# The first layer's kept operands read back in four transfers per half step instead of seven

## The chip, the cores and the metric

The kernel runs on one core of one Trainium2 chip. The metric is the device time of one execution in microseconds (us), lower being better.

## The reference, cut to what matters

Two batch rows of 2048 tokens with 512 features go through three small two-layer networks (two shared ones, one chosen by an id per batch row). A softmax gate weighs the three, the result is added to the tokens, and a second block adds one 512x512 product chosen by a category id.

```
x = hidden_states                                  # [2, 2048, 512]
s0 = relu(x @ swi[0]) @ swo[0]                     # 512 -> 2048 -> 512
s1 = relu(x @ swi[1]) @ swo[1]
eo = relu(x @ wi[type_label]) @ wo[type_label]     # per batch row
w = softmax(relu(concat(eo[:,0], s0[:,0], s1[:,0]) @ g1) @ g2)
x = x + eo * w[:,0] + s0 * w[:,1] + s1 * w[:,2]
x = x + (x @ W[cat_ids] + b[cat_ids])
```

The change touches only how the operands of the first layer (`swi`, `wi`), once prepared, reach TensorE. What is computed stays the same.

## The kernel before, in words

**Tiling.** The 4096 tokens are taken in four supers of 1024 (two blocks of 512). In a super, each of the three networks is worked in four steps of 512 hidden features, so there are 4 x 12 = 48 steps `N`, and each step has two half steps `n = 2N, 2N+1` of 256 hidden features, 96 in all. A half step multiplies 2x2 blocks by a scheme of seven block products in place of eight. Its seven "up" products (`up(n, i)`, i = 0 to 6, L1769) read the operand tile `WU[:, i]`, a high and a low part of 256 columns each, and the token operands `XH`, `XL`. Each product is two groups of three 512-column matmuls (high x high, high x low, low x high), six in all. A step's second layer has seven "down" products of twelve matmuls each, which read `WD`, a ring of four slots, and the hidden operands `HH`, `HL`.

**Operands made once, kept in DRAM.** The seven operands of a half step are sums of weight blocks, split in high and low parts on ScalarE and VectorE. This is done for the steps that `prepared(N)` names: all twelve of super 0, and the four steps of the third network in super 2 (steps 32 to 35), whose weights belong to the other batch row. They are then stored: `keep_up` (L446) writes a half step's operands 0 to 2 and then 3 to 6 from `WU` to `wu_kept`, `keep_down` (L473) writes one `WD` slot to `wd_kept`. The other 32 steps, 64 half steps, read them back: `load_up(n, i)` (L479) brings one operand of 256 KB, `load_down` (L488) one `WD` slot of 512 KB. `WU` has one buffer: operand i of half step n may be overwritten once product i of half step n-1 has ended (`s_up`).

**The order of the work.** Every engine walks the same hand-written loop: for each step `m` seven iterations i. In one iteration TensorE does two up products, j = 2i and 2i+1 (products 0 to 6 of half step `a = 2(m+1)`, then 0 to 6 of `b = a+1`), and one down product (the sum of it is added into `ACC` by VectorE). SyncE issues nearly all transfers, from one queue of instructions and in this order within an iteration: the keeps of up operands if steps are being prepared, the loads that follow up products 2i and 2i+1 (L652 to L655), in the last two steps of a super also a token operand (`load_operand`, L544, and `load_tokens`), then a `load_down`, spills of sums, `keep_down` of slots just made, and the rest. Each issue may be preceded by waits, and while SyncE waits, all that is behind it waits too.

VectorE makes the low parts (`down_low`, L1294, which a `keep_down` waits for through `s_wld`), the low parts of tokens (`token_low`, L1278), sums of hidden blocks and the additions of down products. TensorE waits in `up` for the operand's own semaphore, `s_wu[i]`, one for each of the seven (L1790).

**Where the two regimes meet.** After step 11 and after step 35 prepared steps end and steps with loads begin. During m = 11 and m = 35 SyncE's queue holds the last `keep_down`s of the prepared step between the first `load_up`s. These are the loads for half steps 25, 26 and for 73, 74.

Of the kernel before, what the change touches and what calls it, by code (L numbers as in the profile page):

```python
# [5 lines left out]
F32 = mybir.dt.float32  # L6
# [18 lines left out]
HALVES = 2 * STEPS  # L25
# [11 lines left out]
PRODUCTS = 7  # L37
# [2 lines left out]
UP_BANK = [0, 2, 1, 0, 1, 2, 1]  # L40
UP_ANEW = [True, True, False, False, False, False, False]
EARLY = 3

DN_PAIR = [0, 0, 1, 0, 1, 0, 1]
DN_ANEW = [True, False, False, True, False, False, False]
# [22 lines left out]
def super_of(N):  # L68
    return N // STEPS_SUPER


def net_of(N):
    return N % STEPS_SUPER // STEPS_NET


def slice_of(N):
    return N % STEPS_NET


def prepared(N):  # L80

    return 0 <= N < STEPS and (super_of(N) == 0 or (super_of(N) == 2 and net_of(N) == 2))


def prepared_half(n):
    return prepared(n // 2)


def weight_set(N):
    return net_of(N) * STEPS_NET + slice_of(N) + (STEPS_NET if net_of(N) == 2 and super_of(N) >= 2 else 0)  # L90
# [5 lines left out]
PREP_HALF = [sum(prepared_half(i) for i in range(n)) for n in range(HALVES + 1)]  # L96
# [88 lines left out]
def x_index(s, i):  # L185
    return (X_ORDER if s > 0 else X_ORDER_FIRST).index(i)
# [34 lines left out]
def build(nc, xT, expert_id, category_id, wi, wo, swi, swo, g1, g2, W, bias, out):  # L221
# [6 lines left out]
    wu_kept = nc.dram_tensor("wu_kept", [2 * SETS, P, PRODUCTS, 2, HB], F32, kind="Internal").ap()  # L228
# [6 lines left out]
    with ctx:  # L235
        def sem(name):
            return ctx.enter_context(nc.semaphore(name))
# [3 lines left out]
        def sb(name, shape, dt=F32, at=None):  # L241
            size = 4
            for n in shape[1:]:
                size *= n
            offset = place[0] if at is None else at
            t = nc.alloc_sbuf_tensor_at(name, shape, dt, offset=offset)
            if at is None:
                place[0] += (size + 63) // 64 * 64
            return t
# [14 lines left out]
        WU = sb("WU", [P, PRODUCTS, 2, HB], F32R)  # L264
# [85 lines left out]
        s_wld = sem("down_low_parts")  # L350
        s_wuk = [sem("up_kept_early"), sem("up_kept_late")]
        s_wdk = [sem(f"down_kept_{r}") for r in range(WD_SLOTS)]
        s_wu = [sem(f"up_operand_loaded_{i}") for i in range(PRODUCTS)]
        s_wd = [sem(f"down_operand_loaded_{r}") for r in range(WD_SLOTS)]
        s_up = sem("up_product")
        s_dn = sem("down_product")
# [62 lines left out]
        def _(sp):  # L419
# [26 lines left out]
            def keep_up(n, late):  # L446
                part = slice(EARLY, PRODUCTS) if late else slice(0, EARLY)
                sp.wait_ge(s_wlu, 4 * PREP_HALF[n] + 2 + 2 * late)
                sp.dma_start(wu_kept[2 * weight_set(n // 2) + n % 2, :, part, :, :],
                             WU[:, part, :, :].bitcast(F32)).then_inc(s_wuk[late], 16)  # L450
# [26 lines left out]
                             WD[:, r, :, :, :].bitcast(F32)).then_inc(s_wdk[r], 16)  # L477

            def load_up(n, i):  # L479
                late = int(i >= EARLY)  # L480
                sp.wait_ge(s_up, PRODUCTS * (n - 1) + i + 1)
                sp.wait_ge(s_wuk[late], 16 * PREP_HALF[n])
                if weight_set(n // 2) == 0:
                    sp.wait_ge(s_wsk, 64)
                sp.dma_start(WU[:, i, :, :].bitcast(F32),
                             wu_kept[2 * weight_set(n // 2) + n % 2, :, i, :, :]).then_inc(s_wu[i], 16)

            def load_down(N, i):  # L488
                e = down_of(N, i)
# [14 lines left out]
            def load_tokens(s, j):  # L504

                k, h = ((0, 0), (1, 0), (1, 1), (0, 1))[j]
                if j < 3:
                    if s > 0:
                        sp.wait_ge(s_xlo, PRODUCTS * s)
                        sp.wait_ge(s_gpart, KD * (3 * (s // 2) + (2 if s % 2 else 0)))  # L510
                        for q in range(4):
                            sp.wait_ge(s_ak[q], 16 * (1 if s == 1 else SUPERS - 1))
                        if s > 1:
                            sp.wait_ge(s_out, 16 * SLICES * (s - 1))
                    dst = XS[:, j, :]
                elif s > 0:
                    sp.wait_ge(s_up, PRODUCTS * (2 * STEPS_SUPER * s - 1) + 4)
                    dst = XT[:, 3, :]
                else:
                    dst = first_B21  # L520
                sp.dma_start(dst, xT[s, :, k, h, :]).then_inc(s_xs[j], 16)
# [24 lines left out]
            def load_operand(s, i):  # L546

                q = {1: 0, 4: 1, 2: 2, 5: 3}[i]
                sp.wait_ge(s_up, PRODUCTS * (2 * STEPS_SUPER * s - 1) + i + 1)
                sp.wait_ge(s_ak[q], 16 * s)  # L550
                sp.dma_start(XT[:, i, :], xT_kept[s - 1, q, :, :]).then_inc(s_xt[i], 16)
# [77 lines left out]
            for m in range(STEPS):  # L629
# [4 lines left out]
                for i in range(PRODUCTS):  # L634
# [16 lines left out]
                        keep_up(b + 1, 0)  # L651
                    for j in (2 * i, 2 * i + 1):  # L652
                        n = a + j // PRODUCTS
                        if n + 1 < HALVES and not prepared_half(n + 1):
                            load_up(n + 1, j % PRODUCTS)  # L655
                        if end and j == PRODUCTS + 3:
                            load_tokens(s + 1, 3)
                        elif end and PRODUCTS < j < 2 * PRODUCTS - 1:
                            load_operand(s + 1, j - PRODUCTS)
# [222 lines left out]
        def _(act):  # L882
            def token_high(s, i):
                if s > 0:
                    act.wait_ge(s_up, PRODUCTS * (2 * STEPS_SUPER * s - 1) + i + 1)
                _, _, (sums, fourth), _ = x_from[i]
                if s > 0 and i in s_xt:
                    act.wait_ge(s_xt[i], 16 * s)
                elif sums:
                    act.wait_ge(s_xT, sums)  # L890
                elif fourth:
                    act.wait_ge(s_x4, 1)
                else:
                    act.wait_ge(s_xs[x_loaded[i]], 16 * (s + 1))
                act.activation(XH[:, i, :], x_source(s, i), ACT.Copy).then_inc(s_xhi, 1)  # L895

            def up_high(n, late):
                if n > 2:
                    act.wait_ge(s_up, PRODUCTS * (n - 1) + (PRODUCTS if late else EARLY))
                    act.wait_ge(s_wuk[late], 16 * PREP_HALF[n])  # L900
# [860 lines left out]
        def _(pe):  # L1761
            def product(dst, stationary, moving, start, stop):
                pairs = ((0, 0), (0, 1), (1, 0))
                for j, (a, c) in enumerate(pairs):
                    ins = pe.matmul(dst, stationary[a], moving[c], start=start and j == 0, stop=stop and j == 2,  # L1765
                                    skip_group_check=True)
                return ins

            def up(n, i):  # L1769
                N = n // 2  # L1770
                if i == 0:
                    pe.wait_ge(s_relu, 4 * (n - 1) + 1)
                if i == 1 and n == 2:
                    pe.wait_ge(s_relu, 4 * (n - 1) + 2)
                elif i == 1:
                    pe.wait_ge(s_ev, 2 * (n - 2))
                if i == 2:
                    pe.wait_ge(s_p1, n - 1)
                if i == 4:
                    pe.wait_ge(s_u, n - 1)  # L1780
                if i == 5:
                    pe.wait_ge(s_w, n - 1)
                if i == 6:
                    pe.wait_ge(s_ev, 2 * (n - 2) + 1)
                if n == 2 or n % (2 * STEPS_SUPER) == 0:
                    pe.wait_ge(s_xlo, PRODUCTS * super_of(N) + x_index(super_of(N), i) + 1)
                if prepared_half(n):
                    pe.wait_ge(s_wlu, 4 * PREP_HALF[n] + (1, 2, 2, 3, 4, 4, 4)[i])
                else:
                    pe.wait_ge(s_wu[i], 16 * (n - PREP_HALF[n] + 1))  # L1790
                for q in range(2):
                    cols = slice(q * P, (q + 1) * P)
                    toks = slice(q * TB, (q + 1) * TB)
                    ins = product(ups[UP_BANK[i]][:, :], (WU[:, i, 0, cols], WU[:, i, 1, cols]),
                                  (XH[:, i, toks], XL[:, i, toks]), q == 0 and UP_ANEW[i], q == 1)
                ins.then_inc(s_up, 1)
# [171 lines left out]
```

## Time and profile before

| what | value |
|---|---|
| median of 3 runs | 1934.02 us (1933.66 to 1934.57) |
| the profiled execution, device time | 1933.93 us |
| its span in the profile | 1931.9 us |
| TensorE matmuls busy | 1927.0 us (100%), 8494 of them |
| VectorE busy | 1356.0 us (70%) |
| ScalarE busy | 980.0 us (51%) |
| GpSimd busy | 344.8 us (18%) |
| DMA, all queues | 470.91 MB, mean 244 GB/s |
| DMA queue of SyncE, share of 16 engines | 71.1% |

How to read it: the span runs from the first to the last instruction of the program in the profiled execution; the device time of that same execution is 2.0 us longer. Busy shares are shares of the span. The matmuls are pipelined, and each record lasts longer (389 ns) than the distance from one start to the next, so that "busy" merges them: the idle time of TensorE is what is left between merged stretches.

### The profile page before, as it was taken

To read this page: it belongs to the slowest core of one execution; us is meant where nothing else is said; L and a number is where in the kernel's file an instruction comes from. 1 tells how busy PE (TensorE), PEld (TensorE's weight loads), DVE (VectorE), ACT (ScalarE), POOL (GpSimd) and SP (SyncE) were. 2 spreads that over 40 slices of the span, in tenths; PEclk is the share of its full clock that TensorE was granted. 3 is DMA by queue.
4 is the path that set the end of the run, shared out by engine and by line. 5 is a ranking of instruction groups with operands and counts; after the bars stand their busy time and mean duration, and the time that the engine had idled before them with its cause. 6 is when DMAs were issued, how large, how long until landed. Compare 5 with 4: busy or idle time off the path is not lost. (4 is left out here: it accounts for less than half of the span.)

```text
span 1931.9 us, 25225 instructions
## 1 busy us (share of the span) xinstructions
PE 1927.0 (100%) x8494; PEld 1593.8 (82%) x8494; DVE 1356.0 (70%) x1523; ACT 980.0 (51%) x1441; POOL 344.8 (18%) x245
## 2 busy tenths in 40 slices
PE   9999999999999999999999999999999999999999
PEld 8888888888888888888888888888888888888887
DVE  8999999998666556665655545589976666555566
ACT  7666756766553334444554344456566434344342
POOL 0221132123111111331111111111321112111120
PEclk9999999999999999999999999999999999999999
DMA  6868777867877666886776676587788677656652
GB/s 234 326 251 325 288 293 269 310 242 306 295 250 232 205 217 186 279 290 228 243 253 212 202 225 197 194 287 290 268 304 282 221 234 226 213 183 213 223 158 99
DMA packets 193314, 470.91 MB, mean 244 GB/s; under 512 B 17060, under 2 KB 58020, under 8 KB 187044
## 3 DMA queue, kind: packets, MB, share of 16 engines
q1 hardware_dynamic: 192900, 468.52, 71.1%
q8 instruction: 70, 1.15, 0.2%
q10 hardware_dynamic: 288, 0.79, 0.1%
q14 instruction: 56, 0.46, 0.1%
HBM read 322.44 MB, written 146.80 MB: 243 GB/s over the span
## 5 line engine op out<-in xcount | busy, mean ns | idle before, releaser
L1765 PE MATMUL rps<-HH,WD 128*128 128x512 f32 x2672 | 876.8, 389 | 0.0
L1765 PE MATMUL ups<-XH,WU 128*128 128x512 f32 x2632 | 864.7, 389 | 0.3 <-DMA WU<-wu_kept 0.3
L1765 PEld LDWEIGHTS rps<-HH,WD 128*128 128x128 f32 x2672 | 501.6, 188 | 104.7 <-issue 0.5
L1765 PEld LDWEIGHTS ups<-XH,WU 128*128 128x128 f32 x2632 | 493.9, 188 | 104.5 <-issue 0.9
L1765 PE MATMUL rps<-HL,WD 128*128 128x512 f32 x1336 | 519.9, 389 | 0.0
L1765 PE MATMUL ups<-XL,WU 128*128 128x512 f32 x1316 | 512.2, 389 | 0.0
L802 POOL TENSOR_TENSOR HT<-hid 128x512 f32<-128x512 f32 x81 | 111.2, 1373 | 1349.2 <-PE rps L1765 1349.2
L1311 DVE TENSOR_TENSOR HL<-HT,HH 128x1024 fp32r<-128x1024 f32 x240 | 290.0, 1217 | 11.4 <-ACT HH L988 6.3
L1333 DVE SCALAR_TENSOR_TENSOR ACC<-rps,gw,ACC 128x1024 f32<-128x1024 f32 x126 | 161.5, 1282 | 192.7 <-PE rps L1765 192.5
L1765 PEld LDWEIGHTS rps<-HL,WD 128*128 128x128 f32 x1336 | 250.7, 188 | 52.1
L1765 PEld LDWEIGHTS ups<-XL,WU 128*128 128x128 f32 x1316 | 247.1, 188 | 51.2
L988 ACT ACTIVATE HH<-HT 128x1024 fp32r<-128x1024 f32 x240 | 252.6, 1054 | 24.7 <-DVE HT L802 23.5
L1330 DVE TENSOR_TENSOR ACC<-rps,ACC 128x1024 f32<-128x1024 f32 x124 | 151.1, 1219 | 89.2 <-PE rps L1765 89.0
L964 ACT ACTIVATE HT<-HT 128x512 f32<-128x512 f32 x94 | 59.4, 632 | 269.7 <-DVE HT L1361 269.7
L1311 DVE TENSOR_TENSOR HL<-hid,HH 128x1024 fp32r<-128x1024 f32 x96 | 131.8, 1373 | 20.7 <-ACT HH L988 20.7
L1352 DVE TENSOR_TENSOR hid<-ups,w 128x512 f32<-128x512 f32 x94 | 64.6, 687 | 110.0 <-PE ups L1765 109.8
L956 ACT ACTIVATE hid<-ups 128x512 f32<-128x512 f32 x94 | 55.9, 595 | 109.8 <-PE ups L1765 109.8
L948 ACT ACTIVATE u<-ups 128x512 f32<-128x512 f32 x94 | 56.2, 598 | 102.9 <-PE ups L1765 102.9
L942 ACT ACTIVATE w<-ups 128x512 f32<-128x512 f32 x94 | 55.2, 588 | 97.0 <-PE ups L1765 97.0
L988 ACT ACTIVATE HH<-hid 128x1024 fp32r<-128x1024 f32 x96 | 101.7, 1059 | 3.5 <-PE rps L1765 2.0
L1003 ACT ACTIVATE rps<-rps 128x512 f32<-128x512 f32 x96 | 55.5, 582 | 83.9 <-PE rps L1765 68.6
L936 ACT ACTIVATE ups<-ups 128x512 f32<-128x512 f32 x94 | 54.8, 583 | 76.2 <-PE ups L1765 73.0
(155 smaller groups left out, 1530.9 us busy)
## 6 DMA issues: line engine op xcount, KB each, us to landing
WU<-wu_kept SPq DMA_DIRECT2D x448, 256.0 KB, 3.6
WD<-wd_kept SPq DMA_DIRECT2D x224, 512.0 KB, 3.5
wd_kept<-WD SPq DMA_DIRECT2D x112, 512.0 KB, 4.0
wu_kept<-WU SPq DMA_DIRECT2D x30, 1024.0 KB, 4.9
wu_kept<-WU SPq DMA_DIRECT2D x30, 768.0 KB, 4.1
sums_kept<-ACC SPq DMA_DIRECT2D x28, 512.0 KB, 6.0
MB<-sums_kept SPq DMA_DIRECT2D x28, 512.0 KB, 5.6
XS<-in_x_dram SPq DMA_DIRECT2D x20, 512.0 KB, 6.2
```

What stands on the lines that cost most here:

```text
L802: eng.tensor_tensor(dst, p, q, op).then_inc(s_T[half], 1)
L942: act.activation(w[:, :], ups[2][:, :], ACT.Copy).then_inc(s_w, 1)
L948: act.activation(u[:, :], ups[1][:, :], ACT.Copy).then_inc(s_u, 1)
L956: act.activation(hid[:, 0, half, :], ups[0][:, :], ACT.Relu).then_inc(s_relu, 1)
L964: act.activation(HT[:, 1, n % 2, :], HT[:, 1, n % 2, :], ACT.Relu).then_inc(s_relu, 1)
L988: act.activation(HH[:, i, :, :], src, ACT.Copy).then_inc(s_hhi, 1)
L1003: act.activation(rps[1][:, j, :], rps[0][:, j, :], ACT.Copy).then_inc(s_pc, 1)
L1311: dve.tensor_tensor(HL[:, i, :, :], src, HH[:, i, :, :].bitcast(F32), ALU.subtract).then_inc(s_hlo, 1)
L1330: dve.tensor_tensor(ACC[:, j, :, :], src[:, :, :], ACC[:, j, :, :], ALU.add).then_inc(s_acc, 1)
L1333: dve.scalar_tensor_tensor(out=ACC[:, j, :, :], in0=src[:, :, :], scalar=gw[:, g:g + 1], in1=ACC[:, j, :, :], op0=ALU.mult, op1=ALU.add).t ...
L1352: dve.tensor_tensor(hid[:, 2, half, :], ups[1][:, :], w[:, :], ALU.add).then_inc(s_ev, 1)
L1765: ins = pe.matmul(dst, stationary[a], moving[c], start=start and j == 0, stop=stop and j == 2, skip_group_check=True)
```

## The change

Four semaphores take the place of seven. A transfer now brings operand 0 alone, or operands 1 and 2, 3 and 4, or 5 and 6 together. It is issued where the later operand's load stood, after the later product of the previous half step has ended; the calls for products 1, 3 and 5 are gone. TensorE's wait before product i is for the semaphore of the transfer that brings it.

```diff
+PAIRS = 4
...
-        s_wu = [sem(f"up_operand_loaded_{i}") for i in range(PRODUCTS)]
+        s_wu = [sem(f"up_operands_loaded_{i}") for i in range(PAIRS)]
...
             def load_up(n, i):
                 late = int(i >= EARLY)
+                part = slice(max(i - 1, 0), i + 1)
                 sp.wait_ge(s_up, PRODUCTS * (n - 1) + i + 1)
                 sp.wait_ge(s_wuk[late], 16 * PREP_HALF[n])
                 if weight_set(n // 2) == 0:
                     sp.wait_ge(s_wsk, 64)
-                sp.dma_start(WU[:, i, :, :].bitcast(F32),
-                             wu_kept[2 * weight_set(n // 2) + n % 2, :, i, :, :]).then_inc(s_wu[i], 16)
+                sp.dma_start(WU[:, part, :, :].bitcast(F32),
+                             wu_kept[2 * weight_set(n // 2) + n % 2, :, part, :, :]).then_inc(s_wu[i // 2], 16)
...
                     for j in (2 * i, 2 * i + 1):
                         n = a + j // PRODUCTS
-                        if n + 1 < HALVES and not prepared_half(n + 1):
+                        if n + 1 < HALVES and not prepared_half(n + 1) and j % PRODUCTS % 2 == 0:
                             load_up(n + 1, j % PRODUCTS)
...
                 else:
-                    pe.wait_ge(s_wu[i], 16 * (n - PREP_HALF[n] + 1))
+                    pe.wait_ge(s_wu[(i + 1) // 2], 16 * (n - PREP_HALF[n] + 1))
```

## Rows read from the trace of the kernel before

**Rows 1.** The profile page, part 1, busy time of each engine.
```profile
PE 1927.0 (100%) x8494; PEld 1593.8 (82%) x8494; DVE 1356.0 (70%) x1523; ACT 980.0 (51%) x1441; POOL 344.8 (18%) x245
```

**Rows 2.** Who waited for whom, TensorE (total us, times, longest).
```profile
PE ups L1894 <- POOL ones L854: 1.0, 1, 1.0
PE ups L1765 <- DMA WU<-wu_kept: 0.3, 1, 0.3
PE aps L1765 <- DVE XL L1730: 0.2, 1, 0.2
```

**Rows 3.** Chain of waits: start, us, what; then stretches (PE, PEld, DVE, ACT, POOL; clock, DMA, GB/s).
```profile
1541.67 2.72 PE ups L1765 x12
1544.39 2.72 PE rps L1765 x12
...
1917.80 10.89 PE rps L1765 x48
...
600.00:700.00 100.00, 100.00 (x443) 82.82 (x442) 63.88 (x63) 41.67 (x59) 14.18 (x10) 1.00 0.70 221
1900.00:1932.00 32.00, 28.51 (x125) 22.86 (x123) 16.96 (x20) 3.39 (x4) 0.00 (x0) 0.99 0.18 66
```

**Rows 4.** DMA issues (count, KB, median to landing), then tile WU's landing times.
```profile
WU<-wu_kept SPq DMA_DIRECT2D x448, 256.0 KB, 3.6
WD<-wd_kept SPq DMA_DIRECT2D x224, 512.0 KB, 3.5
...
DMA to landing us min/median/max: 2.6/3.9/11.2
```

**Rows 5.** Who waited for whom, SyncE's queue.
```profile
SPq L496 <- PE rps L1765: 500.4, 217, 5.0
SPq L485 <- PE ups L1765: 390.4, 368, 3.7
SPq L476 <- DVE WD L1298: 277.3, 100, 13.7
```

**Rows 6.** SyncE's issues in order of time, end of step m = 34 and step m = 35.
```profile
1391.33 0.37 SPq L485 DMA_DIRECT2D WU<-wu_kept  x1
1391.79 0.39 SPq L551 DMA_DIRECT2D XT<-xT_kept  x1
1392.29 0.43 SPq L485 DMA_DIRECT2D WU<-wu_kept  x1
...
1407.44 1.28 SPq L485 DMA_DIRECT2D WU<-wu_kept  x2
1422.35 0.32 SPq L476 DMA_DIRECT2D wd_kept<-WD  x1
1422.77 1.21 SPq L485 DMA_DIRECT2D WU<-wu_kept  x2
1424.03 0.47 SPq L476 DMA_DIRECT2D wd_kept<-WD  x1
1424.60 1.58 SPq L485 DMA_DIRECT2D WU<-wu_kept  x2
```

**Rows 7.** TensorE in order of time, half step 73's products 1 and 2.
```profile
1426.15 0.39 PE L1765 MATMUL ups<-XH,WU 128*128 128x512 f32 x1
...
1427.28 0.39 PE L1765 MATMUL ups<-XH,WU 128*128 128x512 f32 x1
...
1427.94 0.47 PE L1765 MATMUL ups<-XH,WU 128*128 128x512 f32 x1 [0.27 <-DMA WU<-wu_kept]
...
1428.25 0.40 PE L1765 MATMUL ups<-XL,WU 128*128 128x512 f32 x1
```

**Rows 8.** Chain of waits at 1422.77; tile WU, the loads issued at 1423.24 and 1424.60.
```profile
1422.77 5.04 DMA WU<-wu_kept
...
L485 SPq DMA_DIRECT2D WU<-wu_kept x1: 732/732/732, 1423.2 to 1423.2; - x1
...
DMA to landing us min/median/max: 5.2/5.2/5.2
...
L485 SPq DMA_DIRECT2D WU<-wu_kept x1: 371/371/371, 1424.6 to 1424.6; - x1
...
DMA to landing us min/median/max: 5.7/5.7/5.7
```

**Rows 9.** Step m = 11: SyncE 464.59 (landing beside it), TensorE from 467.96.
```profile
464.59 1.21 SPq L485 DMA_DIRECT2D WU<-wu_kept  x2
...
DMA to landing us min/median/max: 4.6/4.6/4.6
...
467.96 0.39 PE L1765 MATMUL ups<-XH,WU 128*128 128x512 f32 x1
```

**Rows 10.** VectorE from 1401.86 (21 records up to 1422.84, idle only before the first); TensorE at 1409.60.
```profile
1401.86 1.71 DVE L1282 TENSOR_TENSOR XL<-XT,XH 128x1024 fp32r<-128x1024 f32 x1 [1.49 <-ACT XH L895]
...
1410.31 1.21 DVE L1330 TENSOR_TENSOR ACC<-rps,ACC 128x1024 f32<-128x1024 f32 x1
...
1421.64 0.68 DVE L1298 TENSOR_TENSOR WD<-PDS,WD 128x512 fp32r<-128x512 f32 x1
...
1409.60 0.39 PE L1765 MATMUL rps<-HH,WD 128*128 128x512 f32 x1
```

## The prediction

> **What bounds the kernel now.** The page comes first: matmuls cover 1927.0 of the 1931.9 us, and VectorE follows at 70% [rows 1]. Next, what TensorE waited for: 1.5 us over three waits, one of them for an operand of the change, 0.3 us [rows 2]. Then its pace. Twelve matmuls take 2.72 us in mid-kernel, and 48 take 10.89 us in the last stretch: 227 ns each both times, although the DMA engines are busy 0.70 of the time in the one and 0.18 in the other [rows 3]. So the pace does not hang on the load on the DMA engines, and 8494 x 0.227 = 1928 us is practically the span. The granted clock is 1.00 at mid-kernel and 0.99 at the end. Nothing is to be won but those waits; what the change can do is make an operand late.
>
> **Count.** The 448 loads of 256 KB [rows 4] become 64 of 256 KB and 192 of 512 KB, the bytes unchanged. SyncE saves 192 issues of 0.3 to 0.4 us, which is worth nothing: outside the places below it spends its time waiting for products [rows 5]. Waits of TensorE stay one per product.
>
> **The ordinary half step.** The operands with odd numbers are now fetched one product later, and the even one of a pair is no earlier. Of a pair, the first operand counts, since it is needed first. An iteration is two up products and a down product, 2 x 2.72 = 5.44 us [rows 3]. Operand 1 of half step b is used at the start of iteration 4, and its old contents are free after half step a's product 1, in iteration 0. That leaves one down product and three iterations, 2.7 + 16.3 = 19.0 us. The pair waits for product 2, a down and an up product later: 19.0 - 2.7 - 1.4 = 14.9 us. In the other parity the window is 15.0 us. The median landing is 3.6 us for 256 KB and 3.5 us for 512 KB [rows 4]; the longest of all transfers of `WU`, keeps included, took 11.2 us [rows 4]. So the pair is hidden wherever SyncE issues on time. Cost 0; the cover is these 15 us, and with the cover gone each late us costs TensorE a us.
>
> **Where SyncE does not issue on time.** SyncE waited for VectorE's low parts at `keep_down` for 277.3 us in 100 waits, the longest 13.7 us [rows 5]. Most of it lies in prepared steps, where no load is behind. The exceptions are steps m = 11 and m = 35. At m = 35 (half step 73) loads 0 and 1 are issued in iteration 0, at 1407.44. Then `keep_down` blocks the queue for some 14 us, and goes at 1422.35. Loads 2 and 3 follow at 1422.77 and 1423.24 [rows 6, 8]. Operand 2 lands 5.04 us after its issue, 1427.81, and that is the wait of 0.3 us: product 2's first matmul starts at 1427.94 instead of 1427.28 + 0.23 = 1427.51, so 0.43 us is lost [rows 7, 8]. The change moves load 1 across this `keep_down`, from 1407.44 to 1422.77, joined to load 2. But product 1 starts at 1426.15 [rows 7], 1.36 us ahead of product 2.
>
> **When the pair lands.** No row shows this transfer. Load 3, issued 0.47 us behind load 2, lands 5.2 us after its issue, at 1428.45, 0.64 us behind load 2 [rows 8]. The pair has exactly the bytes of loads 2 and 3 and the same `keep_down` in front, so I take load 3's landing, 1428.4. From below the bound is load 2's own landing, 1427.8 (as if the doubled size cost nothing). From above, the load at 1424.60, with more in front, took 5.7 us [rows 8]; with 0.6 for the doubled size that is 6.3 us, landing 1429.1.
>
> **What comes earlier.** At the end of m = 34 the token operand at 1391.79 stands behind load 1 of half step 72 [rows 6]. The pair now comes behind it, so it has 256 KB less in front, which is up to 0.64 us. VectorE idles 1.49 us for that operand at 1401.86 and then works without a pause to the low part at 1421.64 that frees the `keep_down` [rows 10]. Such a lead passes through all of this but one: the addition at 1410.31 needs a down product whose last matmul runs 1409.60 to 1409.99 [rows 10], so 0.3 us is left. I take 0.3; the bounds are 0 and 0.6.
>
> **The sum.** At m = 35: landing 1428.4 - 0.3 = 1428.1, 0.13 us to the matmul as now (1427.81 to 1427.94), start 1428.2. Stall 1428.2 - 1426.15 = 2.1 us, less the 0.43 already lost: +1.7 us. At m = 11 the same queue: load 2 issued at 464.59 landed 4.6 us later, 469.2, just in time; the pair lands 0.6 later and 0.3 earlier, 469.5, start 469.6; product 1 starts at 467.96 [rows 9]. Stall 1.7 us, less about 0.1 for the slower matmul there now: +1.6 us. Sum +3.3 us. The pairs 3-4 and 5-6 behind them are not late: pair 3-4 goes at 1424.60 and lands, by the load of that moment, 5.7 us later at 1430.3, while product 3, an up product and a down product behind 1427.94, starts near 1432.0, and later still by the stall. Nothing gives a stall back: VectorE gets time that it does not need, and all later loads shift with TensorE. For the clock I allow nothing, since no stretch read shows less than 0.99 [rows 3]; the stall of now slows only the next matmul, by 0.08 us (1427.94 to 1428.25) [rows 7]. The profiled execution took 1933.93 us, 0.1 below the median of the runs: 1933.93 + 3.3 = 1937.2 us. With the low ends (landing as load 2, 0.3 earlier) the stalls are about 0.6 shorter each: +2.0, 1936.0. With the high ends (6.3 us, no lead) it is 2.6 + 3.0 = +5.6, 1939.5.
>
> A page speaks for the change: the Trainium skill, DMA: Bandwidth & Descriptors, under Bandwidth (Measured), advises batching transfers to 1 MiB or more, and under Anatomy of one DMA gives each a fixed cost of about 2 us. By that rule three fixed costs per half step go, so the pair would come sooner than two loads. No row agrees: two loads 0.47 us apart land 0.64 us apart [rows 8], so fixed parts overlap in the queue.
>
> **Rivals.** A measurement of this kernel can tell 0.2%, 3.9 us, from no change.
>
> (a) Slower by more: the lead of 0.3 us does not arrive, or the queue in front of the pair is longer, so that it lands at load 3's time or after it. Price: 1428.45 + 0.13 - 1426.15 - 0.43 = 2.0 and 469.8 + 0.13 - 467.96 - 0.1 = 1.9, so +3.9 at least and +5.6 at most: 1937.9 to 1939.5. It decides once the pair lands 0.3 us later than I take it at both places. For it: all transfers at these moments stand in a full queue. Against it: VectorE's idle 1.49 us is plainly that token transfer's. Chance 0.33.
>
> (b) Hidden: the pair lands before product 1, or VectorE's lead is much larger, since the order in front of it changes. It needs a landing 2 us sooner than taken, under 3.4 us from issue, where the rows show 4.6 and 5.04. Time 1934.0, down to 1933.4 if the 0.5 us of now goes too. Chance 0.09.
>
> (c) Faster: TensorE's pace is held back by the transfers of small rows after all, and a share of it returns. By [rows 3] the pace at a DMA share of 0.18 is that at 0.70, so I give it 0.04; one per cent of the pace would give 1915. By the page's rule, too, no more than the 0.5 us of waits could return, since TensorE has no other idle time for a load; its time would be 1933.4.
>
> (d) That the change does not do what it says can hardly be: call, slice and semaphore index agree.
>
> **How the numbers follow.** Forecast (two stalls, +2.0 to +3.8) 0.54, (a) 0.33, (b) 0.09, (c) 0.04. Both the forecast and (b) lie within 0.2%: same 0.63. Slower 0.33, faster 0.04. The likeliest time is 1937.2 us. The range takes the forecast and (a) nearly whole and leaves out (c), most of (b) and the end of (a): 1934.6 to 1939.3.
>
> **What would show it.** TensorE's waits for `WU` rise from 0.3 to some 4 us, in two waits near 468 and 1426, each before the first matmul of a product 1 and none before product 2. In SyncE's queue one load of 256 KB stands at 1407.4, and the pair behind the `keep_down` at about 1422.5 (1422.8 would be (a)), landing about 5.6 us later. The addition at 1410.31 starts at 1410.0, with a short idle time in front. Between these places the matmuls keep 2.72 us per twelve. The prediction is wrong if there is no wait at those places, if waits appear in ordinary half steps, or if the pace changes.

## The result and the profile after

Twelve executions of the changed kernel took 1939.89 us in the median (1937.86 to 1941.31), twelve of the kernel before 1934.23 us (1933.66 to 1935.08). The ratio is 1.0026 with a 95% interval of 1.0018 to 1.0033, so slower, by about 5 us (5.7 us between the two medians). The profiled execution took 1938.38 us (span 1936.3 us), 1.5 us under the median, and that difference turned out to be part of the answer: the times of the changed kernel lie in two groups. The four executions with a mean granted TensorE clock of 1.000 took 1937.86 to 1938.60 us, the eight with 0.999 took 1939.63 to 1941.31 us.

The profile page of the changed kernel, parts 1 and 5 (busy, mean ns of one, then idle before and its releaser):

```profile
PE 1927.6 (100%) x8494; PEld 1593.4 (82%) x8494; DVE 1359.5 (70%) x1523; ACT 980.2 (51%) x1441; POOL 344.7 (18%) x245
...
L1770 PE MATMUL ups<-XH,WU 128*128 128x512 f32 x2632 | 864.7, 389 | 4.0 <-DMA WU<-wu_kept 3.9
```

Who waited for whom, TensorE, changed kernel:

```profile
PE ups L1770 <- DMA WU<-wu_kept: 3.9, 2, 2.2
...
PE rps L1815 <- ACT WD L1053: 0.4, 1, 0.4
```

The busy time is that of before [rows 1] to within a microsecond, and so is the matmul (389 ns). What is new is idle time in one group, two waits for `WU` with 3.9 us in place of one with 0.3 [rows 2]. Here are the two places, TensorE in order of time in the changed kernel, last matmul of a down product and then product 1:

```profile
467.86 0.39 PE L1770 MATMUL rps<-HH,WD 128*128 128x512 f32 x1
469.92 0.47 PE L1770 MATMUL ups<-XH,WU 128*128 128x512 f32 x1 [1.67 <-DMA WU<-wu_kept]
...
1428.07 0.39 PE L1770 MATMUL rps<-HH,WD 128*128 128x512 f32 x1
1430.69 0.47 PE L1770 MATMUL ups<-XH,WU 128*128 128x512 f32 x1 [2.23 <-DMA WU<-wu_kept]
```

A matmul normally starts 0.23 us after its forerunner, so product 1 was due at 468.09 and at 1428.30: stalls of 1.83 and 2.39 us. The bracket shows less, since it counts only idle time behind the modelled end of the last matmul. Less what stood there before (0.43 and 0.08), that is 3.7 of the 4.45 us between the two profiled executions. Another 0.3 us is the wait at L1815 near the start, which lasts anything from nothing (the kernel before, `own_25`) to 1.8 us (`own_73`) in the profiles of this document, and 0.4 us is a short wait for VectorE near 1520.

SyncE's queue around the two places, changed kernel:

```profile
464.26 0.32 SPq L479 DMA_DIRECT2D wd_kept<-WD  x1
464.69 0.37 SPq L490 DMA_DIRECT2D WU<-wu_kept  x1
...
1409.74 0.39 SPq L490 DMA_DIRECT2D WU<-wu_kept  x1
...
1424.64 0.32 SPq L479 DMA_DIRECT2D wd_kept<-WD  x1
1425.07 0.37 SPq L490 DMA_DIRECT2D WU<-wu_kept  x1
```

One load at 1409.74 where there were two [rows 6], and operand 1 now comes after the blocking `keep_down`, fifteen us later. Elsewhere nothing is late. DMA issues and a mid-kernel stretch of the changed kernel (columns as in [rows 4] and [rows 3]):

```profile
WD<-wd_kept SPq DMA_DIRECT2D x224, 512.0 KB, 3.4
WU<-wu_kept SPq DMA_DIRECT2D x192, 512.0 KB, 4.3
...
600.00:700.00 100.00, 100.00 (x443) 82.81 (x442) 65.21 (x65) 41.41 (x58) 15.05 (x10) 1.00 0.69 221
```

A pair takes 4.3 us to land in the median where a single one took 3.6, and 443 matmuls in 100 us is what it was.

### The profile page after: what moved, and what is told of

It is laid out like the page before. It is cut to its first block and busy times, and to the rows that moved or that the text cites. A ratio compares the mean times of both kernels' runs of the same rounds, so it can differ in the third digit from the quotient of the medians.

```text
span 1936.3 us, 24841 instructions
## 1 busy us (share of the span) xinstructions
PE 1927.6 (100%) x8494; PEld 1593.4 (82%) x8494; DVE 1359.5 (70%) x1523; ACT 980.2 (51%) x1441; POOL 344.7 (18%) x245
```

## The experiments

Every kernel ran with the kernel before on the same chip. Ratios are to it, with 95% intervals.

**The changed kernel again**, for its profile and its spread.

> The changed kernel, once more, for its profile and the spread of its times. First theory (two stalls, and after them in some executions a fall of TensorE's clock): executions fall in two groups, near 1938.3 us with a granted clock of 1.000 and near 1940 us with 0.999; the two waits for WU are 1.7 and 2.2 us in both. Rival (something spread over the kernel, at 64 half steps): the times are one group, and the twelve matmuls of an ordinary product pair take more than 2.72 us.

Median 1938.15 us against 1933.77, ratio 1.0023 (1.0014 to 1.0033). Six executions with clock 1.000 took 1936.85 to 1938.47 us, four with 0.999 took 1939.48 to 1940.76: two groups again, as expected. The profiled one is of the second kind, 1940.46 us. Its stretches, then TensorE in order of time behind its second stall:

```profile
1426.00:1430.00 4.00, 3.72 (x17) 2.75 (x15) 4.00 (x6) 3.49 (x5) 0.00 (x0) 1.00 0.82 219
1430.00:1432.00 2.00, 0.34 (x2) 0.33 (x3) 2.00 (x3) 1.15 (x3) 0.00 (x0) 1.00 0.98 389
1432.00:1435.00 3.00, 3.00 (x9) 2.35 (x8) 2.41 (x3) 0.60 (x1) 0.00 (x0) 0.50 1.02 419
1435.00:1440.00 5.00, 5.00 (x23) 4.07 (x22) 0.96 (x1) 0.60 (x1) 0.91 (x1) 0.96 1.02 399
```

```profile
1429.33 0.39 PE L1770 MATMUL rps<-HH,WD 128*128 128x512 f32 x1
1431.66 0.47 PE L1770 MATMUL ups<-XH,WU 128*128 128x512 f32 x1 [1.94 <-DMA WU<-wu_kept]
1431.97 0.58 PE L1770 MATMUL ups<-XL,WU 128*128 128x512 f32 x1
1432.35 1.06 PE L1770 MATMUL ups<-XH,WU 128*128 128x512 f32 x2
1433.20 0.63 PE L1770 MATMUL ups<-XL,WU 128*128 128x512 f32 x1
...
1435.62 0.40 PE L1770 MATMUL ups<-XL,WU 128*128 128x512 f32 x1
```

After the wait the granted clock is 0.50, the lower of the two levels (1.2 GHz), and matmuls follow each other at 0.43 us (0.85 for two, 1432.35 to 1433.20) in place of 0.23. Nine matmuls take 1435.62 - 1431.97 = 3.65 us where 2.04 would do, so this costs 1.6 us more. The first stall of the same execution (469.00 to 471.35 less one step of 0.23, 2.12 us) left the clock alone. The Trainium skill, TensorE: Matmul & The Clock Gate, Part 1, says that a TensorE that was idle is throttled to 1.2 GHz until it has been active again. The trace agrees at the second stall (2.10 us, 0.50 after it) and not at the first (2.12 us, 1.00 after it), so the length of the stall alone does not decide it here.

**Operand 1 alone in its old place, at the two half steps only** (`own_both`). All other half steps keep their pairs. `load_alone` is the old load of operand 1, with a semaphore of its own, on which product 1 waits.

```diff
+SPLIT = (25, 73)
...
-                part = slice(max(i - 1, 0), i + 1)
+                part = slice(2, 3) if i == 2 and n in SPLIT else slice(max(i - 1, 0), i + 1)
...
+                        if n + 1 in SPLIT and j % PRODUCTS == 1:
+                            load_alone(n + 1)
```

> The changed kernel, but for half steps 25 and 73 operand 1 comes alone, in its old place ahead of the keep_down, and operand 2 alone in its old place; the 62 other half steps keep their pairs. Two stalls: the time is that of the kernel before, 1934.2 us within 0.4, with the wait of 0.3 us before product 2 of half step 73 back, and no execution has a clock under 1.000. Rival (pairs cost at every half step, by their later fetch or their size): 1937 us or more stays, of the 5.7 us at most 4.2 go.

Median 1934.06 us against 1933.77, ratio 1.0001 (0.9992 to 1.0010), no execution under 1.000. TensorE's only wait for `WU` is that of before:

```profile
...
PE ups L1782 <- DMA WU<-wu_kept: 0.2, 1, 0.2
```

The 62 half steps with pairs cost 0.3 us by the medians, which cannot be told from nothing (the interval is 1.5 us below to 1.9 us above); the 4.4 us of the changed kernel on this chip come from the two.

**One place each.** `SPLIT = (25,)` leaves the stall at half step 73, `SPLIT = (73,)` that at 25.

> The changed kernel, but at half step 25 operands 1 and 2 come apart, operand 1 ahead of the keep_down; half step 73 keeps its pair, so one stall is left, of 2.0 to 2.4 us, less the 0.4 us that stands there anyway. Two stalls that add: 1934.0 + 1.8 = 1935.8 us where the clock stays at 1.000, and 1.7 us more, 1937.5 us, in the executions with 0.999, a third to a half of them. Rival (the fall of the clock needs both stalls, or is no work of them): no execution with 0.999, or as many as with both.

> The mirror of it: half step 25 keeps its pair and stalls 1.8 to 2.1 us, half step 73 has its operands apart. Two stalls that add: 1935.9 us with the clock at 1.000, 1937.6 us with 0.999. The gains of this and of the other, taken together, make the whole of what the change lost. Rival (one place starts what the other pays for): one of the two kernels is at 1934 us and the other at 1938 us.

Against 1933.79 us: the first 1936.35 us, ratio 1.0013 (1.0004 to 1.0022), the second 1936.14 us, 1.0012 (1.0003 to 1.0021). Each loses 2.4 to 2.6 us, together 4.9, between the 4.4 us of the changed kernel in its second set of runs and the 5.7 of the first. So the places add, and one stall alone can bring the clock down (against the rival that both are needed): four of eleven executions of the first have 0.999 (1937.42 to 1937.88 us), two of the second, where two more at 1937.42 and 1937.81 us show 1.000 in three digits. Six of 22 with one stall against 12 of 22 with both fits falls that come from each stall by itself, but the numbers are too small to show it. The profiled execution of the second is one with a fall, behind a stall of 2.00 us at half step 25 that ended at 470.39. There the clock stayed up for about a microsecond after TensorE had resumed, 0.88 being the mean of the first stretch:

```profile
470.00:472.00 2.00, 1.61 (x6) 1.38 (x7) 2.00 (x3) 0.00 (x0) 0.00 (x0) 0.88 1.03 412
472.00:474.00 2.00, 2.00 (x6) 1.53 (x5) 1.26 (x2) 0.60 (x1) 0.00 (x0) 0.50 1.03 422
474.00:480.00 6.00, 6.00 (x25) 4.92 (x25) 1.22 (x1) 1.50 (x3) 2.10 (x2) 0.92 1.02 363
```

**The pair asked for ahead of the keep_down** (`early`).

```diff
+                        if m in (11, 35) and j == 2:
+                            continue
                         if n + 1 < HALVES and not prepared_half(n + 1) and j % PRODUCTS % 2 == 0:
                             load_up(n + 1, j % PRODUCTS)
+                        if m in (11, 35) and j == 0:
+                            load_up(n + 1, 2)
```

> The changed kernel with its pairs, but in steps 11 and 35 the pair 1-2 is issued in iteration 0, ahead of the keep_down that blocks the queue, once product 2 has ended. Two stalls by queue position: the pair is asked for some 10 us sooner, both waits go, and so does the 0.3 us wait of the kernel before: 1933.6 us, 0.3 to 0.7 below before. Rival (the size of a transfer or its wait for the later product is what costs): a stall of a us or more stays, 1936 us or more.

Median 1933.62 us against 1933.77, ratio 0.9997 (0.9988 to 1.0006), so equal; the 0.3 to 0.7 us below before that I expected are too small to be seen. SyncE's queue in step 35 and TensorE's waits:

```profile
1408.14 3.91 SPq L490 DMA_DIRECT2D WU<-wu_kept  x2
1423.04 1.52 SPq L479 DMA_DIRECT2D wd_kept<-WD  x2
1424.68 1.56 SPq L490 DMA_DIRECT2D WU<-wu_kept  x1
```

```profile
PE rps L1819 <- ACT WD L1057: 1.2, 1, 1.2
PE ups L1903 <- POOL ones L863: 1.0, 1, 1.0
PE aps L1774 <- DVE XL L1739: 0.2, 1, 0.2
```

Same sizes, same wait for product 2, and no wait for `WU` at all: it is the place in the queue that cost.

**Place without size** (`late1`): the kernel before, with operand 1 of the two half steps moved behind the `keep_down`, 256 KB as ever.

```diff
+                        if n + 1 in (25, 73) and j % PRODUCTS == 1:
+                            continue
+                        if n + 1 in (25, 73) and j % PRODUCTS == 2:
+                            load_up(n + 1, 1)
```

> The kernel before with its seven transfers; only operand 1 of half steps 25 and 73 is issued after the keep_down, directly ahead of operand 2, each still 256 KB. By place alone: operand 1 lands where operand 2 did (4.6 and 5.0 us after the issue), stalls of 1.4 and 1.8 us before product 1, operand 2 then in time: 1934.2 + 1.4 + 1.4 = 1937.0 us, plus up to 1.8 us in executions in which the clock falls. By size (the rival: only joining them stalls): 1934.5 us at most.

Median 1936.44 us, ratio 1.0013 (1.0004 to 1.0022), no execution under 1.000 (1935.35 to 1937.39). TensorE at both places:

```profile
468.01 0.39 PE L1769 MATMUL rps<-HH,WD 128*128 128x512 f32 x1
469.51 0.47 PE L1769 MATMUL ups<-XH,WU 128*128 128x512 f32 x1 [1.11 <-DMA WU<-wu_kept]
...
1427.49 0.39 PE L1769 MATMUL rps<-HH,WD 128*128 128x512 f32 x1
1428.44 0.47 PE L1769 MATMUL ups<-XH,WU 128*128 128x512 f32 x1 [0.56 <-DMA WU<-wu_kept]
```

Stalls of 1.27 and 0.72 us before product 1, the second shorter than the 1.8 I expected, since operand 1 landed 4.0 us after its issue there and not 5.0. Less the 0.51 us that stood there before, they make 1.5 us, while the profiled execution (1935.81 us) lies 2.0 us above the median of before, and the median 2.7 us above it. That this is near the 2.8 of the expectation is luck: the stalls that were seen do not add up to it, and what the slower executions add was not profiled. The move costs a stall without any joining; joining adds to it (1.83 and 2.39). No execution here shows a mean clock under 1.000.

**Another grouping** (`group01`): 0-1, 2-3, 4-5, 6.

```diff
-                part = slice(max(i - 1, 0), i + 1)
+                part = slice(i - 1 if i % 2 else i, i + 1)
...
-                        if n + 1 < HALVES and not prepared_half(n + 1) and j % PRODUCTS % 2 == 0:
+                        if n + 1 < HALVES and not prepared_half(n + 1) and j % PRODUCTS in (1, 3, 5, 6):
...
-                    pe.wait_ge(s_wu[(i + 1) // 2], 16 * (n - PREP_HALF[n] + 1))
+                    pe.wait_ge(s_wu[i // 2], 16 * (n - PREP_HALF[n] + 1))
```

> The changed kernel with another grouping, still four transfers: 0-1, 2-3, 4-5 and 6 alone, each after its later product. Now operand 1 stands ahead of the keep_down, and the pair 2-3 behind it lands 0.6 us after operand 2 alone would, while product 2 is due 1.36 us later than product 1. By the place of a pair's first operand: stalls of 0.6 us (half step 25) and 1.0 us (73) before product 2, none before product 1, 1933.8 + 0.6 + 0.6 = 1935.0 us, and no fall of the clock. Rival (any pair behind the keep_down costs what 1-2 did): 1937 us or more.

Median 1935.10 us against 1933.78, ratio 1.0006 (0.9997 to 1.0015), all eleven at 1.000. TensorE, last matmul of product 1 and first of product 2:

```profile
469.22 0.39 PE L1770 MATMUL ups<-XH,WU 128*128 128x512 f32 x1
470.14 0.47 PE L1770 MATMUL ups<-XH,WU 128*128 128x512 f32 x1 [0.53 <-DMA WU<-wu_kept]
...
1428.13 0.39 PE L1770 MATMUL ups<-XH,WU 128*128 128x512 f32 x1
1429.54 0.47 PE L1770 MATMUL ups<-XH,WU 128*128 128x512 f32 x1 [1.03 <-DMA WU<-wu_kept]
```

Stalls of 0.7 and 1.2 us, before product 2 this time. As many transfers as in the change, of the same sizes, for 1.3 us in place of 4.4 to 5.7: what matters is when the first operand of the pair behind the `keep_down` is due.

**A longer stall** (`longer`): the pair one `keep_down` further back.

```diff
+                        if m in (11, 35) and j == 2:
+                            continue
...
                     for k in made_after(past, which):
                         keep_down(k // PRODUCTS, k % PRODUCTS)
+                    if m in (11, 35) and i == 1:
+                        load_up(a + 1, 2)
```

> The changed kernel with the pair 1-2 of half steps 25 and 73 one keep_down further back in the queue: issued some 1.2 us later with 512 KB more in front, so that each stall grows from about 2.1 to about 3.5 us. If a longer stall makes the fall of the clock surer: every execution has 0.999 or less, and the time is 1934.0 + 3.5 + 3.1 + one or two times 1.7 = 1942.3 to 1944.0 us. Rival (the fall comes or not whatever the length of the stall): the executions stay split as before, with a median of 1941 us or less.

Median 1943.95 us, five executions from 1941.56 to 1945.69, ratio 1.0050 (1.0036 to 1.0064), all with 0.997 to 0.999. In the profiled one the first stall is 3.3 us, near the 3.5 that I had worked out, and the second 4.6 us, a microsecond more. The second:

```profile
1430.00:1434.00 4.00, 1.66 (x8) 1.04 (x6) 4.00 (x6) 3.19 (x6) 0.00 (x0) 1.00 0.99 277
1434.00:1440.00 6.00, 3.88 (x9) 3.13 (x10) 2.53 (x3) 0.60 (x1) 0.00 (x0) 0.51 1.01 391
```

Here the clock was at its lower level before TensorE resumed (1436.12). So falls go with the length of the stalls: a mean clock of 0.999 is absent from the 33 executions of `own_both`, `early` and `late1` (stalls up to 1.3 us), is there in part of those with stalls near 2 us, and in all five of this kernel. It does not take such a stall, though: one of the 92 executions of the kernel before shows 0.999 too, at 1936.41 us, the slowest of them. It was not profiled, so what lowered the clock there is open.

**The lead that did not come** (`xt_after`): at the end of steps 10 and 34 the pair goes ahead of the first token operand (and no more at j = 9).

```diff
...
+                        if m in (10, 34) and j == 8:
+                            load_up(n + 1, 2)
```

> The changed kernel, but at the end of steps 10 and 34 the pair 1-2 of half steps 24 and 72 is issued ahead of the first token operand, not behind it, so that this operand lands 1.3 us later. The forecast's term (VectorE passes a lead or a delay of that operand on, up to 0.3 us of lead): VectorE reaches the addition after its third token operand later, the keep_down that frees the queue goes 0.6 us or more later, both stalls grow by that. Rival (a collision of VectorE with GpSimd takes the lead away whatever the operand's landing): the keep_down goes within 0.2 us of where it does in the changed kernel, measured from the same product of TensorE, and the stalls stay at 1.7 to 2.4 us.

One execution, 1937.91 us, clock 1.000. SyncE's queue:

```profile
464.42 0.32 SPq L479 DMA_DIRECT2D wd_kept<-WD  x1
```

Product 1 was due at 468.06 here, so the `keep_down` goes 3.64 us ahead of it; in the changed kernel 468.09 - 464.26 = 3.83, in the kernel before 467.96 - 464.16 = 3.80. At half step 73 the figures are 3.68 us here and 3.66 in the changed kernel. VectorE's start on the token operand moved by 1.5 us between the two paired kernels and the queue by 0.2 and 0.0, so the rival has it. The stalls were 2.30 and 2.00 us; the first grew by 0.5 although the queue moved by only 0.2, as the pair landed 5.4 us after its issue and not 5.1. VectorE's rows show why the queue hardly moved. The kernel before, then the changed kernel, then `xt_after`:

```profile
443.67 1.72 DVE L1282 TENSOR_TENSOR XL<-XT,XH 128x1024 fp32r<-128x1024 f32 x1 [1.48 <-ACT XH L895]
...
448.73 1.22 DVE L1282 TENSOR_TENSOR XL<-XT,XH 128x1024 fp32r<-128x1024 f32 x1
449.86 1.21 DVE L1330 TENSOR_TENSOR ACC<-rps,ACC 128x1024 f32<-128x1024 f32 x1
```

```profile
442.98 1.28 DVE L1287 TENSOR_TENSOR XL<-XT,XH 128x1024 fp32r<-128x1024 f32 x1 [0.67 <-ACT XH L900]
...
447.61 2.32 DVE L1287 TENSOR_TENSOR XL<-XT,XH 128x1024 fp32r<-128x1024 f32 x1
449.85 1.21 DVE L1335 TENSOR_TENSOR ACC<-rps,ACC 128x1024 f32<-128x1024 f32 x1
```

```profile
444.45 2.30 DVE L1291 TENSOR_TENSOR XL<-XT,XH 128x1024 fp32r<-128x1024 f32 x1 [2.19 <-ACT XH L904]
...
448.99 1.21 DVE L1291 TENSOR_TENSOR XL<-XT,XH 128x1024 fp32r<-128x1024 f32 x1
450.12 1.21 DVE L1339 TENSOR_TENSOR ACC<-rps,ACC 128x1024 f32<-128x1024 f32 x1
```

With the change VectorE starts 0.7 us earlier and is still ahead at 447.61. Then the next token operand takes 2.32 us instead of 1.22, and the addition starts at 449.85 as before. GpSimd runs 512-column operations beside it that stretch too, first the kernel before, then the changed one:

```profile
443.02 1.29 POOL L810 TENSOR_TENSOR PDS<-PDR 128x512 f32<-128x512 f32 x1
```

```profile
443.14 2.28 POOL L815 TENSOR_TENSOR PDS<-PDR 128x512 f32<-128x512 f32 x1
```

In these rows the engine that starts first takes its short time and the other is stretched: VectorE at 442.98 (1.28 us) ahead of GpSimd at 443.14 (2.28), GpSimd at 443.02 (1.29) ahead of VectorE at 443.67 (1.72), and in `xt_after` GpSimd at 444.38 (1.28) ahead of VectorE at 444.45 (2.30). At half step 73 the lead goes at once. The token operand of 1401.86 before [rows 10] reads in the changed kernel:

```profile
1403.59 2.27 DVE L1287 TENSOR_TENSOR XL<-XT,XH 128x1024 fp32r<-128x1024 f32 x1 [1.27 <-ACT XH L900]
```

Product 1 is due 2.15 us later there (1428.30 against 1426.15), so VectorE starts 0.42 us early by that measure; the operation then takes 2.27 us in place of 1.71 and ends 0.14 us late, which is what the `keep_down` shows. That the collision is the cause of the lost lead fits all three traces; it was not tried without GpSimd.

**A version better than both?** The kernel before with its operands 2 and 3 asked for early (`before_early`), and the paired one again.

> The kernel before with its seven transfers; in steps 11 and 35 operands 2 and 3 are issued in iteration 0, ahead of the keep_down. The only wait of TensorE for WU goes: 0.3 to 0.5 us below the kernel before, 1933.4 us, the same as with pairs asked for early. Rival (pairs themselves give or take something): it differs from the paired kernel by 0.5 us or more.

> The paired kernel whose pair 1-2 is issued ahead of the keep_down, once more on the same chip as the two others: 1933.4 us, within 0.3 us of the seven transfers with the same early issue; lower than the kernel before by 0.2 to 0.5 us if the waits it lacks are all that differs. Rival: at or above the kernel before.

1933.82 us and 1933.73 us against 1933.78, ratios 1.0000 (0.9991 to 1.0009) and 0.9999 (0.9990 to 1.0008). Neither profile has a wait for `WU` left. All three are equal within what can be measured: both expected gains of 0.2 us or more are not seen, and the scatter of the start (0 to 1.8 us at the wait for ACT `WD` alone, from profile to profile) is larger than the 0.5 us at stake.

## Why the prediction was right or wrong

- **TensorE is the bound and its pace does not hang on transfers**: right. 443 matmuls in 100 us before and after, at a DMA share of 0.70 and 0.69, and `own_both` with 62 of 64 half steps paired is within 0.3 us of before.
- **Ordinary half steps cost nothing**: right as far as the times can tell, by the same run and by `early`, which has all its pairs.
- **Two stalls, at half steps 73 and 25, before product 1, none before product 2**: right, in place and kind; `own_25` and `own_73` show that they add.
- **When the pair lands**: right. 464.69 to 469.78 is 5.1 us (taken 5.2), 1425.07 to 1430.55 is 5.5 us (taken 5.6).
- **The lead of 0.3 us**: wrong. It was 0.03 us at half step 25, and at 73 the `keep_down` went 3.66 us ahead of product 1's due time where it had gone 3.80 us ahead, so 0.14 us later. The step that failed was "Such a lead passes through all of this but one": VectorE's operations were taken at fixed durations, and one of them was stretched, 2.32 us in place of 1.22 at half step 25 and 2.27 in place of 1.71 at 73. With that the stalls were 1.83 and 2.39 us against 1.7 and 2.1, and the sum +3.7 against +3.3. This is the upper edge of the forecast (+3.8), just short of case (a) (+3.9), whose sign came: the pair's issue, 1425.07 less the 2.15 us, is 1422.9.
- **"For the clock I allow nothing"**: wrong, and the larger error. I argued from a trace whose only stall for an operand was 0.43 us; with stalls of about 2 us, 12 of 22 executions of the changed kernel have a mean clock of 0.999. A fall costs 1.6 us in the profile. The two groups lie farther apart, 2.8 us in the second set; the rest is not accounted for (a second fall, or longer stalls in those executions, would do it).
- **The numbers**: executions at 1.000 lie at 1936.85 to 1938.60 us, those of the first set all above the forecast of 1937.2 (1937.86 and more), those of the second around it; the median over all, 1939.89, lies above it and above the range's end of 1939.3 as an absolute time, while the ratio 1.0026 on 1934.02 gives 1939.0, inside it. That it is inside is in part luck: the range was made wide for a late pair, and most of what lies beyond the forecast is the clock, which stood in no term. The likeliest verdict was no change within 0.2%; the ratio is just beyond, with an interval that begins below it. Rival (a), at 0.33, named that side and range, but only half the mechanism: no lead, yes; a clock, no.
- **Rivals (b), (c)**: the waits behind the 0.5 us of (b) go only with the early issue, which the change does not do, and even then the gain is not seen in the times. The rule that larger transfers pay has nothing to pay out here, where no load is late but at two places, and there the pair came later.

## What to carry to other kernels

When transfers are joined, the join inherits the latest place of its parts in the issuing queue and the earliest due time: look for the one spot where something blocks the queue between those places, because the ordinary spots with 15 us of slack say nothing about it. If the join is wanted, issue it ahead of what blocks. A stall of TensorE of about 2 us is not priced by its length alone: add a share of a clock fall (1.6 us in the one profile worked out here), which also splits a kernel's times in two groups, so that one profiled execution can look a microsecond or two better than the median.

## What was not expected of the hardware

The granted clock fell to 0.50 behind a stall of 2.10 us and stayed at 1.00 behind others of 2.12 and 2.39 us, in the same kernel, and after a stall of 2.00 us it fell only when TensorE had been at work again for a microsecond. VectorE's 1024-column operation on the token operand took 1.2 or 2.3 us and GpSimd's 512-column one 1.29 or 2.28 us, the later of two that overlapped being the long one, enough to swallow a lead of 0.7 us and most of a delay of 0.8 us (443.67 to 444.45, but 449.86 to 450.12).
